# Three loads of the joint stage move from SyncE's DMA queue to ScalarE's

## Time and profile before

| | |
|---|---|
| median of 3 executions | 1350.73 us (1350.36 to 1351.67) |
| the profiled execution, its own time | 1349.87 us |
| its span in the trace | 1347.8 us |
| busy in the span: PE, DVE, ACT, POOL | 88%, 68%, 49%, 39% |
| the joint stage | 807 to 1033 us |
| TensorE's granted clock, mean of the span | 0.935 |
| q1 (SyncE's DMA queue) | 235.14 MB |
| q10 (ScalarE's DMA queue) | 1.14 MB, all at the start of the kernel |

### The profile page before, as it was taken

The page is one execution under the profiler, slowest core; times in us unless marked ns, Lnnn a source line. Parts: engine busy times, 40 slices in busy tenths (PEclk is TensorE's granted clock), DMA queues, the critical chain, the costliest instruction groups (busy, mean ns, idle before and its releaser), DMA issues. The chain is left out here.

```text
span 1347.8 us, 25076 instructions
## 1 busy us (share of the span) xinstructions
PE 1182.2 (88%) x9030; PEld 872.9 (65%) x9030; DVE 911.4 (68%) x2166; ACT 664.5 (49%) x1120; POOL 524.5 (39%) x448
## 2 busy tenths in 40 slices
PE   5899999999999997599999966999992399935998
PEld 5788888888888885476666523566551288932443
DVE  5667767766777775344554332999994699976874
ACT  3344334444443443224434342666774299657992
POOL 1233333333333333248768731476663000002352
PEclk9999999999999998699999987999996599966999
DMA  6222322332222216295887889999923589734994
GB/s 231 80 72 98 115 96 97 107 113 104 94 94 94 94 64 217 98 360 186 301 312 282 293 325 336 370 339 329 325 110 83 109 231 408 317 131 190 418 365 149
DMA packets 127601, 274.25 MB, mean 203 GB/s; under 512 B 44145, under 2 KB 55313, under 8 KB 120849
## 3 DMA queue, kind: packets, MB, share of 16 engines
q1 hardware_dynamic: 113840, 235.14, 49.1%
q0 software_dynamic: 10688, 36.71, 7.7%
q10 hardware_dynamic: 2976, 1.14, 0.3%
HBM read 155.26 MB, written 109.31 MB: 196 GB/s over the span
## 5 line engine op out<-in xcount | busy, mean ns | idle before, releaser
L1958 PE MATMUL p_z<-qT,w1T 128*128 128x256 bf16 (+1 forms) x1152 | 114.2, 262 | 14.4 <-DMA qT<-p_q 14.3
L1958 PEld LDWEIGHTS p_z<-qT,w1T 128*128 128x128 bf16 x1152 | 102.5, 99 | 25.8 <-DMA qT<-p_q 14.4
L2423 POOL DMA_DIRECT2D p_y<-residual x32 | 26.7, 835 | 230.1 <-POOLq L113 198.6
L379 PE MATMUL p_M<-p_ctxTh,early 128*128 128x256 f32 x512 | 101.0, 291 | 1.9 <-DVE early L712 1.9
L1136 DVE COPY p_selT<-p_sel 128x512 f32<-128x512 f32 x64 | 44.3, 692 | 83.5 <-PE p_sel L989 83.5
L379 PE MATMUL p_M<-p_xnTh,early 128*128 128x256 f32 x512 | 99.0, 287 | 0.6 <-DVE p_V L785 0.6
L2444 PE MATMUL p_o<-w2T,p_Gq 128*128 128x512 bf16 x384 | 86.6, 387 | 6.0 <-DVE p_Gq L2491 6.0
L379 PEld LDWEIGHTS p_M<-p_ctxTh,early 128*128 128x128 f32 x512 | 82.8, 193 | 2.3 <-issue 2.3
L379 PEld LDWEIGHTS p_M<-p_xnTh,early 128*128 128x128 f32 x512 | 80.7, 188 | 3.6 <-issue 3.6
L636 POOL TENSOR_TENSOR p_rs<-p_ve,p_mhalf 128x2 f32<-128x2 f32 x32 | 22.3, 698 | 153.2 <-DVE p_ve L702 153.1
L379 PE MATMUL p_M<-early,p_ctxTh 128*128 128x512 f32 x256 | 81.5, 399 | 0.0
(11 more groups left out here) (373 smaller groups left out, 3266.1 us busy)
## 6 DMA issues: line engine op xcount, KB each, us to landing
inter_d<-p_stage SPq DMA_DIRECT2D x64, 512.0 KB, 4.5
p_rows<-inter_d SPq DMA_DIRECT2D x32, 1024.0 KB, 9.4
activations<-hid SPq DMA_DIRECT2D x20, 1024.0 KB, 7.0
p_cin<-in_ctx_dram SPq DMA_DIRECT2D x32, 512.0 KB, 5.3
xparts<-p_parts SPq DMA_DIRECT2D x16, 768.0 KB, 3.3
activations<-third SPq DMA_DIRECT2D x12, 1024.0 KB, 6.6
hid<-activations SPq DMA_DIRECT2D x12, 1024.0 KB, 14.4
p_xin<-in_x_dram SPq DMA_DIRECT2D x16, 512.0 KB, 4.2
```

The source lines that it names most:

```text
L379: mm = pe.matmul(out, left[a][:, c, lcols], right[e][:, c, rcols], start=(k == 0), stop=(k == len(terms) - 1))
L1958: mm = pe.matmul(bank, w1T[:, c, fc * P:(fc + 1) * P], qT[:, bass.ds(first, tiles), c, :], start=(c == 0), stop=(c == C - 1))
```

## The change

The three loads are defined in ScalarE's program instead of SyncE's, with the same waits, and called there: for batch 0 ahead of everything, the residual of batch i+1 behind `hidden`, context and mask of batch i+1 behind `e_turned`. SyncE keeps rows and stores in their order.

```diff
@@ SyncE
-            def load_x(b):
-                if b >= XD:
-                    wait_all(sp, "hh_done", b - XD + 1)
-                    sp.wait_ge(s[f"x_out{b % XD}"], 16 * (b // XD))
-                sp.dma_start(xy[b % XD][:, :, :], x_mid[b]).then_inc(s[f"x_in{b % XD}"], 16)
-
-            def load_ctx(b):
-                if b >= CD:
-                    wait_all(sp, "O_full", b - CD + 1)
-                sp.dma_start(cin[b % CD][:, :, :], ct[b]).then_inc(s[f"c_in{b % CD}"], 16)
-
-            def load_mask(b):
-                if b >= 2:
-                    sp.wait_ge(s["mask_done"], b - 1)
-                sp.dma_start(mk[b % 2][:, :, :].rearrange("p t k -> p (t k)"), mask[b].broadcast_to([P, S])).then_inc(s[f"m_in{b % 2}"], 16)
...
             load_rows(0, 0)
             load_rows(0, 1)
-            load_x(0)
-            load_ctx(0)
             load_rows(1, 0)
-            load_mask(0)
             for i in range(STEPS):
                 if live(i + 1):
                     load_rows(i + 1, 1)
-                    load_x(i + 1)
-                    load_ctx(i + 1)
                 if live(i + 2):
                     load_rows(i + 2, 0)
-                if live(i + 1):
-                    load_mask(i + 1)
...
@@ ScalarE
+            def load_x(b):
+                if b >= XD:
+                    wait_all(act, "hh_done", b - XD + 1)
+                    act.wait_ge(s[f"x_out{b % XD}"], 16 * (b // XD))
+                act.dma_start(xy[b % XD][:, :, :], x_mid[b]).then_inc(s[f"x_in{b % XD}"], 16)
...
+            load_x(0)
+            load_ctx(0)
+            load_mask(0)
             act.wait_ge(s["const_in"], 32)
             act.activation(tgf[:, :], gf_s[:, :], ACT.Tanh).then_inc(s["tanh_done"], 1)
             act.activation(tgx[:, :], gx_s[:, :], ACT.Tanh).then_inc(s["tanh_done"], 1)
...
                     hidden(i - 4, 1)
+                if live(i + 1):
+                    load_x(i + 1)
                 if live(i - 1):
                     ctx_out(i - 1, 0)
...
                     e_turned(i - 2)
+                if live(i + 1):
+                    load_ctx(i + 1)
+                    load_mask(i + 1)
                 if 0 <= i - STEPS + EST_ROUNDS:
```

More of the change, by code:

```diff
@@ L1429, in estimate, with load_ctx, load_mask @@
                 act.activation(minus_t[:, :], higher[:, :], ACT.Identity, bias=minus_t[:, :], scale=-2.0 ** (1 - r)).then_inc(s["est_own"], 1)
+            def load_x(b):
[3 more added lines that the diff above has]
+                act.dma_start(xy[b % XD][:, :, :], x_mid[b]).then_inc(s[f"x_in{b % XD}"], 16)
+            def load_ctx(b):
+                if b >= CD:
+                    wait_all(act, "O_full", b - CD + 1)
+                act.dma_start(cin[b % CD][:, :, :], ct[b]).then_inc(s[f"c_in{b % CD}"], 16)
+            def load_mask(b):
+                if b >= 2:
+                    act.wait_ge(s["mask_done"], b - 1)
+                act.dma_start(mk[b % 2][:, :, :].rearrange("p t k -> p (t k)"), mask[b].broadcast_to([P, S])).then_inc(s[f"m_in{b % 2}"], 16)
+            load_x(0)
+            load_ctx(0)
+            load_mask(0)
             act.wait_ge(s["const_in"], 32)
```

## The result

The changed kernel takes 1365.52 us, the median of 5 runs (1362.96 to 1370.83), against 1350.46 (1349.06 to 1351.67, 5 runs) for the kernel before: a ratio of 1.0116, with an interval of 1.0096 to 1.0136. It is slower, as forecast, but by 15 us and not by 4.3, and outside the range.

The account below looks back on a forecast made before the run. TensorE was taken to bound the joint stage's middle, load order mattering only in the 36 us fill. Fill +3.0 and steady steps +0.2, +0.3, +0.8 gave +4.3 us on 1350.73: 1355.0 us, range 1349.5 to 1361.0.

Parts of the forecast that it names:

- Item 2: Fill: four ScalarE loads for batches 1 and 2 slip between packets of rows tile (0,1), delaying batch 0's additions, +4.6 us.
- Item 1: Fill: batch 0's residual, context and mask, issued as the stage opens, fit a near-idle DMA gap; rows start 0.5 us late.
- item 3: Fill: context 0 is in early, shortening the way from addition to `turn_xn`, -0.4 us; later rows (1,1) cost 0.
- item 4: Fill, step 2: TensorE's idling before `scatter(2,1)` goes, as those rows no longer queue behind residual and context, -0.8 us.
- item 5: Fill: TensorE's clock grant relative to the delayed work, from half speed recovered to up to 2 us lost; taken as -0.4 us.
- items 6 and 7: Steady steps: issue time on ScalarE, +0.2 us for context and mask in steps 13 and 14, +0.3 for the residual.
- Item 8: Steady steps: ScalarE's residual load waits for an older store's landing, margin 0.5 to 0.9 us, some late, +0.8 us.
- rival B: Steps 5 to 14: the store's landing becomes ScalarE's wait in every step, 1364 us, milder forms 1359 to 1362; chance 0.13.
- Rival A: Fill: the issuing queue doesn't matter or early loads cost the rows nothing, 1349.5 to 1351 us, up to 1352; chance 0.30.

Follow-up runs that it names:

- experiment 2: The changed kernel with SyncE issuing the store of batch i-4 ahead of rows (i+2,0) instead of behind them, six residual buffers: 1355.78 us.
- experiment 1: The changed kernel with seven residual buffers instead of six: 1355.39 us.
- experiment 7: The changed kernel with seven residual buffers, ScalarE holding residual, context and mask of batch 1 and residual 2 until batch 0's second rows tile landed: 1354.74 us.
- experiment 5: The changed kernel with seven residual buffers, ScalarE waiting for the gates before its first residual, context and mask loads: 1352.96 us.
- experiment 3: The changed kernel with the residual loaded by SyncE again at its old place, context and mask staying on ScalarE: 1352.8 us.
- experiment 4: The changed kernel with only the residual on ScalarE, context and mask back on SyncE at their old places: 1361.51 us.
- experiment 9: The changed kernel, six residual buffers, with the residual's load moved behind `e_turned`, just before the context's: 1356.27 us.
- experiment 10: Experiment 9 with ScalarE also waiting for the gates before its first loads and for batch 0's second rows tile before batch 1's loads: 1350.42 us.
- experiment 8: The kernel before, with only the two gate loads issued by ScalarE at the start of the stage: 1349.48 us.
- experiment 11: Experiment 10 with a step's three loads placed behind the quantile estimate's round instead of ahead of it: 1353.51 us.
- experiment 6: The kernel before with a seventh residual buffer and nothing else: 1349.5 us.

## Why the prediction was wrong, and where it was right

**The fill: right in size, in part by luck.** Forecast +3.0 us, measured +3.2 in the one profile of the changed kernel; with the same order of loads experiments 2 and 1 have +4.6 and +6.2. Item 2 put the second scatter at 823.5; it came at 825.25, 1.7 us later. Its 4.2 us for four loads between the rows' packets were 3.6 by experiment 7. The DMA queues of the changed kernel from 821 to 824 us (packets, MB, share of 16 engines) show the sharing on which it rests:
```profile
q10 hardware_dynamic: 208, 0.78, 66.0%
q1 hardware_dynamic: 208, 0.42, 37.0%
```
208 packets of each, and ScalarE's have two thirds of the bytes, as the earlier trace rows had said. Item 1 was wrong: it let three loads slip into the gap that the gates' tiny packets leave, for 0.5 us of delay, and did not ask what the gap's owner would lose. The gates landed 3.8 us later (experiment 5 undoes it), and the first scatter came at 819.83 instead of 816.17. What made the total come out is the way from the second scatter's start to the first `attend`: 24.9 us before and 21.7 after, where items 3 to 5 had 1.6 us of gain. The context that is in early gives 0.5 (item 3: 0.4), the idling before `scatter(2,1)` 0.9 (item 4: 0.8), and the clock the rest, 1.8, where item 5 had 0.4. The two windows, of the kernel before and the changed one, end just before 829, from where both have the full clock (the earlier trace rows and the windows above):
```profile
815.00:828.60 13.60, 9.81 (x42) 3.94 (x43) 3.53 (x8) 3.29 (x6) 2.02 (x5) 0.50 1.04 396
...
824.00:828.80 4.80, 3.55 (x17) 1.85 (x18) 1.45 (x3) 0.53 (x1) 0.27 (x1) 0.50 1.04 390
```
The clock was granted at the same moment although the work came later, the first of item 5's three cases. From `turn_xn` (824.83 in the earlier trace rows) to `scatter(1,1)` it is 5.7 us before and 3.9 after:
```profile
830.49 1.06 PE L1293 MATMUL p_s<-p_rows,p_permT 128*32 128x512 f32 x8
...
830.68 0.66 PE L1275 MATMUL p_T<-p_ident,p_xn 128*128 128x128 f32 x4 [1.50 <-ACT p_xn L1355]
...
834.58 1.06 PE L1270 MATMUL p_s<-p_rows,p_permT 128*32 128x512 f32 x8
```
So items 1 and 2 were 1.7 us too low and item 5 promised 1.4 too little; that they cancelled is luck, and in experiment 1 the clock came later and they did not.

**The steady steps: items 6 and 7 small, as said.** An issue of the residual on ScalarE costs no period anything (126.35 us in experiment 1 against 126.36 before; +0.3 was forecast). Context and mask ahead of the estimate, +0.2 forecast, are the likeliest cause of the 1.0 to 1.3 us of the last four periods in experiments 1, 2, 3 and 5, since experiment 4, without them, has none of it; but 9 and 10 have the same order of them and lose nothing in the sum, so what decides there is not shown.

**Item 8 is the step that failed.** It charged 0.8 us for ScalarE's wait for the store. In the profile of the changed kernel the five waits come to 14.1 us (11.1 in four until 985, and 3.0 in one behind it), and their periods are 15.1 us longer than before. Experiments 1 and 2 take the wait away in two ways, and by the medians the kernel is 9 us faster each time. The direction of the argument was right, including the place, the instructions stopped and the point of decision (a landing later than 7.1 us after issue). The size of one term was wrong, the landing: 6.5 us, a sum for a queue that is free but for one rows tile. In the changed kernel the stores from 858 to 985 us landed so (min/median/max), and in the kernel before, to 980 us, so:
```profile
DMA to landing us min/median/max: 7.0/7.7/11.7
```
```profile
DMA to landing us min/median/max: 5.8/7.3/8.4
```
The ten stores for which ScalarE waits landed after 7.0 to 9.9 us; the 11.7 is a later one, for which it doesn't. The median of before, 7.3, stood in the earlier trace rows, beyond the point of decision already. It was argued down, because context, residual and mask would no longer stand ahead of the store in its queue. They left the queue, but not the engines: the same bytes move in the same 11.49 us. In a step with a wait, 901.8 to 911.9 us, the DMA engines' busy tenths and queues are
```profile
DMA  9961615959777999969999999999999999999999
...
DMA packets 1345, 3.24 MB, mean 321 GB/s; under 512 B 66, under 2 KB 106, under 8 KB 1345
## 3 DMA queue, kind: packets, MB, share of 16 engines
q1 hardware_dynamic: 1077, 2.40, 70.7%
q10 hardware_dynamic: 268, 0.84, 20.7%
```
A store of 0.5 MB saw 3.24 MB go by, its own included. In the step ahead of it, from 890.3 to 897.8 us, whose period is the usual 11.50, they are
```profile
DMA  0000070736898963797789799999999999989999
...
q10 hardware_dynamic: 8, 0.02, 0.8%
```
Here the engines had run dry when the store was issued (890.71), since the wait in the step before had held the residual back, and it landed after 7.0 us. This fits the lost time, which comes in every second step: a stall lets the DMA engines catch up, the next step is on time and fills them again. It is a reading of one trace, though, and the landing events of the same stores limit it. These are the 16 updates of the store's semaphore in the trace, one for each DMA engine, and the last is the landing. In all ten, thirteen of the sixteen had done so 6.3 to 7.2 us after the issue, near item 8's 6.5; in the four with the long stalls the last one or two came after 9.4 to 9.9. So what item 8 lacked is the spread to the last engine, and why one falls behind by 2 us and more stays open. Such stragglers come without any stall too: in experiment 10, at the full pace, one store took 9.8 us. Starts of `attend` in the changed kernel, from 881.44: periods of 14.22, 11.50, 15.70, 11.48, 12.21, 11.71 and 15.53 us.

So rival B was the case, in five of the ten steps and with 0.7 to 4.2 us each, where its text had 1.0 us in each of ten. Its sign stood in the prediction, periods above 11.8 and ScalarE waiting for the store. (The other signs: the second scatter came 0.25 us behind the stretch named, the first `attend` 3.2 us later, and q10 carries 18.9 MB more.) It had been given 0.13 and its full price was left out of the range. That price was itself too low, because it took a landing of 8.1 us where 9.5 to 9.9 came in the long stalls, and because it charged the wait alone. The period with a wait of 3.28 us from 881.44 kept the full clock (the window 888.5 to 891.9 above), though TensorE idled 2.51 us before its `turn_xn`, and is 2.7 us too long; the three with the 0.50 windows shown above, after 2.42, 2.25 and 2.67 us of idling, are 4.2, 4.0 and 3.4 us too long (the last against the 12.5 of its place before). So the clock adds about 1.2 us (0.7 to 1.5) to a stall of the same length, when it falls. This is a comparison of four periods within one trace, not an experiment of its own; experiment 4, whose clock stayed full, fits it: 23.9 us of waits cost its 11 periods less (10.3 us) than 11.1 us of waits cost those of the changed kernel (11.9). But they are spread over nine steps, and how much of each a step absorbs is not separated from the clock.

**Rival A** falls with the fill: the first scatters are later by 3.7 and 6.4 us. The Trainium skill's DMA: Bandwidth & Descriptors, section Issuing engines are not separate DMA queues, by which moving an issue saves sequencer time and nothing else, describes experiment 10 well (ratio 1.0011) and the change badly (1.0116). The queue as such is worth 0.3 to 2.7 us here; what an issue waits for, with what stands behind it, is worth 8 to 9 us, and the transfers that it falls between some 3 us or more in the fill.

**Nothing tried beats the kernel before.** Its middle is at TensorE's pace (35.00 of 35.00 us), and of the variants tried none is faster. In the fill experiment 8 shows 0.7 us at most, which the times don't confirm.

## What to carry to other kernels

Before a DMA issue is moved to a compute engine's queue, ask what the issue waits for: SyncE waited 63 us in all for the stores and it cost nothing, while waits of 2 or 3 us in some steps cost 8 to 9 us on ScalarE, since everything behind them stops and TensorE's clock can fall with it. Take the landing time for the margin from the measured landings of the same transfer (median and worst), not from a sum over what will be ahead in its own queue, because other queues' transfers take their share of the DMA engines (q10 20.7% beside q1's 70.7% above) and the slowest engine decides. If the margin is under a few microseconds (0.5 to 0.9 in item 8, where the landings reached 3.4 us beyond the 6.5), move the issue to a place in the step that is reached later, or give it a buffer more; both restored the pace here to 0.01 us.

## What the hardware showed that was not expected

- A load of half a kilobyte suffered much from the second queue: 8.2 us to landing instead of 4.4, and the rows behind it in its own queue were late with it (first scatter 12.5 us after the identity's issue, 8.9 before).
- The last of the 16 engines decides when a store has landed. By the landing events of the store issued at 902.22, the first engine was done 6.4 us after the issue, fourteen after 6.9, the next after 7.8 and the last after 9.65.
- A 128x2 operation of VectorE took 2.30 us where it began beside a 128x1024 multiplication on GpSimd (2.35 us; both ended within 0.02 us of each other), and 0.17 us in most other places (nearly every profile has one or two places where it takes 1.7 to 2.3). Where it does so in the next to last period, that period is 10.5 us (the changed kernel and experiments 1, 2, 3, 5, 9, 10 and 11); where not, it is 9.6 (the kernel before and 4, 6, 7 and 8). That is a coincidence seen in thirteen profiles and no experiment took it away, so its cost is not shown.
- Of four idle stretches of 2.3 to 2.7 us on TensorE, three were followed by work at a granted 0.50 and one was not; the prices of these alike stalls, 2.7 to 4.2 us, differ by over a microsecond.
- In the fill the full clock came at the same moment in the kernel before and the changed one (0.50 until 828.6 and 828.8, then 1.00) and some 7 us later in experiment 1 (0.50 until 835.9), whose program differs by one buffer.
